# Retrieval layer of a four-stage model kernel: last product in three reduced passes, part of the vector work moved to GpSimd

## The chip, the cores and the metric

The kernel runs on one core of one Trainium2 chip. The metric is the device time of one launch in microseconds. Before the change it was 1889.96 us, the median of three runs (1884.06 to 1893.62).

## What is computed

The model has four layers over 2048 tokens of width 256, each followed by an addition and a layer normalisation. The change touches only the fourth, a retrieval layer ("product keys"). Cut to its core:

```
h   = (silu(x @ W_up.T + b_up)) @ W_down.T + b_down          # 2048 x 128
sim = q(h) against 2 x 8 sets of 45 keys                      # q(h) = h @ W_q.T
sx, ix = top 8 of the first set of each head; sy, iy = of the second
all_scores = sx[:, None] + sy[None, :]                        # 8 x 8 candidates for each head
sc, pk  = top 8 of the 64 candidates; indices = ix * 45 + iy of the chosen
z   = silu((h . down_embed[indices]) * softmax(sc))           # 64 values for each token
out = sum over the 64 of z * up_embed[indices]                # up_embed: 2048 x 256, f32
x   = layernorm(x + out)
```

## The kernel before, in words

The tokens are taken in 16 tiles of 128. Nothing is gathered by address. The 2048 experts are laid out as a grid of 16 rows by 128 columns, and an index is split into its column b and its row a. TensorE first multiplies h with the whole of down_embed (`fill_z`, `lower_z`, kept as three bf16 parts in `z`), picks the 64 columns of each token by products with one-hot matrices `is_b` (`gather`), picks the row with `of_a` on VectorE (`weigh`), and after the silu goes the way back: `spread` holds the 64 weights, each cut into three bf16 parts (`c_parts`), placed at its row by `of_a`; `scatter` multiplies them with the one-hot `of_b`; `flip` transposes; ScalarE copies the result to `W`, a 128 x 2048 f32 matrix of weights for the tile (`copy_W`); and `product` multiplies `W` with `up` (the up_embed table in SBUF), 16 products of 128 x 128 by 128 x 256 in f32, which add up in `ps_out`.

The order is written out by hand as one loop over I on each engine, with the stages of several tiles in flight. On TensorE, iteration I does: gather(I), a piece of h for a later block (`private_product`), product(I-1, part 0), select(I), the fill of z for tile I+1 with product parts 1 to 3 of tile I-1 in between, scatter(I), scores(I+3), flip(I), and, in the first iterations, another piece of h (`rise_product`). On VectorE, iteration I does:

```
marks(I)           # is_b x4 (L2147), of_a (L2138), of_b x2 (L2131)
normalize(I + 1)   # softmax sum, reciprocal, weights w (L2260 to L2264)
top_eights(I + 2)  # 16 MAX8 (L2191)
keep_h(I + 2)
weigh(I)           # masked x2 (L2160), row sum (L2163), times w (L2165)
places_of(I + 2)   # 16 FIND_INDEX8 (L2197), then cand (L2200) and the cast of the places (L2205)
cut(I)             # c_rest, c_parts (L2170 to L2174), then spread x4 (L2182)
bests(I + 2)       # 8 MAX8 (L2211), soft (L2215), 8 FIND_INDEX8 (L2219)
look_up(I + 2)     # 12 small instructions, among them hit and found (L2225 to L2256)
add_out(I - 1)
```

Engines wait for each other by counting semaphores. The instructions named above as is_b, of_a, of_b, spread, hit and found read bf16 from SBUF and write bf16 to SBUF. GpSimd has no instruction in this layer. The first token block's h comes from `private_phase`, which ends before the retrieval block begins; the tables (`down`, `up` and smaller ones) are loaded during it.

Of the kernel before, what the change touches and what calls it, by code (L numbers as in the profile page):

```python
# [1644 lines left out]
def private_phase(nc, M, D, h, wk, wu, wd, bu, bd, load_tables):  # L1645


    with scope(nc, "pv") as s:
# [9 lines left out]
        h_product, k_product = s.sem("h_product"), s.sem("k_product")  # L1658

        with nc.Block() as block:  # L1660
# [31 lines left out]
            @block.scalar  # L1692
            def _(act):
                act.wait_ge(k_product, 1)
                for n in range(2):
                    nc.scalar.activation(wk[:, n * RHEADS * KEYS:(n + 1) * RHEADS * KEYS],
                                         ps_k[n][:, 0:RHEADS * KEYS], ACT.Copy)
                act.wait_ge(up_loaded, 4 * 16)
                for m in range(UPT):
# [9 lines left out]
def retrieval_phase(nc, M, D):

    with scope(nc, "re") as s:
# [60 lines left out]
        W = s.sb("W", [P, ROWS, P])  # L1772
        masked = s.sb("masked", [P, ROWS, TWIN])
# [7 lines left out]
        lifted = s.sb("lifted", [P, QT, P])  # L1781
# [4 lines left out]
        def lane(q):  # L1786
            return wheel[:, q * BLK:(q + 1) * BLK]
# [10 lines left out]
                 "b_stored b_spread is_b_ready of_b_ready of_a_ready z_filled z_ready gathered masked_ready "  # L1798
                 "zs_ready c_ready spread_ready scattered W_ready pull selected lift flipped up_product up_ready h_used h_kept out_product added spread root normed step").split()
# [19 lines left out]

        def cut_order(j, n):  # L1820

            return (j // 2) * 2 * PARTS + n * 2 + j % 2 + 1

        with nc.Block() as block:
# [23 lines left out]
            def _(pe):  # L1848
# [268 lines left out]
            def _(dve):  # L2117
# [18 lines left out]
                def of_as(T):  # L2136
                    after(dve, "spread_ready", T * 2)
# [17 lines left out]
                def weigh(T):  # L2155
                    dve.wait_ge(S["of_a_ready"], T + 1)
                    for c in range(2):
                        after(dve, "selected", T * 2 + c + 1)
                        t = slice(c * HALF_TWIN, (c + 1) * HALF_TWIN)
                        nc.vector.tensor_tensor(masked[:, :, t], lane(c).rearrange("p (t a) -> p a t", a=ROWS),  # L2160
                                                of_a[:, :, t], ALU.mult).then_inc(S["masked_ready"], 1)
                    dve.wait_ge(S["masked_ready"], T * 2 + 2)
                    then(nc.vector.tensor_reduce(zs[:, :], masked[:, :, :].rearrange("p a t -> p t a"), AX.X, ALU.add))  # L2163
# [3 lines left out]
                def cut(T):  # L2167
# [6 lines left out]
                    then(nc.vector.tensor_tensor(c_parts[:, 2, :], c_rest[:, :], c_parts[:, 1, :], ALU.subtract))  # L2174
                    now()
                    dve.wait_ge(S["step"], 1)
                    shape = [TWIN, PARTS, ROWS, HALF_TWIN]
                    for c in range(2):
                        t = slice(c * HALF_TWIN, (c + 1) * HALF_TWIN)
                        for half in range(2):  # L2180
                            p = slice(half * TWIN, (half + 1) * TWIN)
                            last = nc.vector.tensor_tensor(  # L2182
                                spread[p, :, half * ROWS:(half + 1) * ROWS, t],
                                of_a[p, :, t].unsqueeze(1).broadcast_to(shape),
                                c_parts[p, :, t].unsqueeze(2).broadcast_to(shape), ALU.mult)
                        last.then_inc(S["spread_ready"], 1)

                def top_eights(T):
# [3 lines left out]
                    then(last)  # L2192

                def places_of(T):
                    now()
# [3 lines left out]
                    both = top[:, :, :].rearrange("p (h a) k -> p h a k", a=2)  # L2199
                    nc.vector.tensor_tensor(  # L2200
                        cand[:, :, :, :],
                        both[:, :, 0, :].unsqueeze(3).broadcast_to([P, RHEADS, K_HEAD, K_HEAD]),
                        both[:, :, 1, :].unsqueeze(2).broadcast_to([P, RHEADS, K_HEAD, K_HEAD]), ALU.add)
                    dve.wait_ge(S["sim_read"], T + 1)
                    then(nc.vector.tensor_copy(place16[:, :, :, :],  # L2205
                                               place[:, :, :].rearrange("p (h a) k -> p a k h", a=2)))
# [16 lines left out]
                def look_up(T):  # L2223
# [11 lines left out]
                    now()  # L2235
                    then(nc.vector.tensor_tensor(found[:, :, :, :].rearrange("p a i (k h) -> p (a i) k h", h=RHEADS),
# [192 lines left out]
```

## Time and profile before

| | |
|---|---|
| profiled execution, device time | 1888.3 us |
| span of the profiled execution, first to last instruction | 1886.5 us |
| median of the timed runs | 1889.96 us |
| TensorE busy over the span | 1696.0 us (90%) |
| VectorE busy over the span | 1162.3 us (62%) |
| ScalarE busy over the span | 879.1 us (47%) |
| GpSimd busy over the span | 555.1 us (29%), none of it in the retrieval layer |
| retrieval loop, first MEMSET of VectorE to the last instruction | 1321.7 to 1886.5 us |

The span is cut into engines and lines of the kernel; a row of the trace gives the start of an instruction (or of a run of like instructions), its length, its engine and line, and what it writes and reads. The shares of the whole span mix four layers with different limits, so the retrieval layer has to be read from its own stretch. The profiled execution lies 1.7 us under the median of the timed runs.

### The profile page before, as it was taken

To read this page: it belongs to the slowest core of one execution; us is meant where nothing else is said; L and a number is where in the kernel's file an instruction comes from. 1 tells how busy PE (TensorE), PEld (TensorE's weight loads), DVE (VectorE), ACT (ScalarE), POOL (GpSimd) and SP (SyncE) were. 2 spreads that over 40 slices of the span, in tenths; PEclk is the share of its full clock that TensorE was granted. 3 is DMA by queue.
4 is the path that set the end of the run, shared out by engine and by line. 5 is a ranking of instruction groups with operands and counts; after the bars stand their busy time and mean duration, and the time that the engine had idled before them with its cause. 6 is when DMAs were issued, how large, how long until landed. Compare 5 with 4: busy or idle time off the path is not lost. (4 is left out here: it accounts for less than half of the span.)

```text
span 1886.5 us, 41922 instructions
## 1 busy us (share of the span) xinstructions
PE 1696.0 (90%) x16332; PEld 1321.6 (70%) x16332; DVE 1162.3 (62%) x2902; ACT 879.1 (47%) x1576; POOL 555.1 (29%) x467
## 2 busy tenths in 40 slices
PE   7999999999999897699997987667899999899998
PEld 6888888888888686487766664224477786677777
DVE  1034434444343476223799989990898798799994
ACT  4433233333333343355776665432465555456563
POOL 2223423333342600730677878540000000000000
PEclk9999999999999899799999988897999999999999
DMA  2000000000000300622544544344212112112120
GB/s 95 19 1 26 21 4 25 25 11 14 25 22 3 114 1 3 215 89 70 169 134 145 158 127 113 105 103 127 91 47 92 47 47 86 64 47 93 59 92 24
DMA packets 74788, 129.98 MB, mean 69 GB/s; under 512 B 13520, under 2 KB 40272, under 8 KB 72408
## 3 DMA queue, kind: packets, MB, share of 16 engines
q1 hardware_dynamic: 73532, 126.09, 21.4%
q10 hardware_dynamic: 1116, 1.98, 0.3%
q8 instruction: 93, 1.52, 0.3%
q14 instruction: 47, 0.39, 0.1%
HBM read 125.28 MB, written 2.77 MB: 68 GB/s over the span
## 5 line engine op out<-in xcount | busy, mean ns | idle before, releaser
L1285 POOL TENSOR_TENSOR mo_sb_bx<-mo_sb_dtx,mo_sb_bs 128x1024 f32<-128x1024 f32 x64 | 153.3, 2396 | 87.9 <-DMA mo_sb_bs<-mo_bc 34.8
L541 POOL TENSOR_TENSOR g_sb_squares_sum<-g_sb_squares_sum,at_sb_qT 128x512 f32<-128x512 f32 x64 | 81.8, 1278 | 309.9 <-ACT at_sb_qT L472 309.9
L2045 ACT ACTIVATE re_sb_z<-re_ps_misc 128x512 bf16<-128x512 f32 x192 | 107.4, 594 | 128.9 <-PE re_ps_misc L1859 85.9
L1472 DVE TENSOR_TENSOR mo_ps_h<-mo_ps_h,mo_sb_gate 128x512 f32<-128x512 f32 x100 | 69.6, 696 | 116.1 <-ACT mo_ps_h L1321 116.0
L1480 DVE TENSOR_TENSOR_SCAN mo_ps_a<-mo_ps_a,mo_sb_bx 128x512 f32<-128x512 f32 x104 | 123.1, 1216 | 0.8 <-POOL mo_sb_bx L1285 0.5
L1946 PE MATMUL re_ps_out<-re_sb_up,re_sb_W 128*128 128x256 f32 x512 | 122.1, 383 | 0.9 <-ACT re_sb_W L2030 0.9
L503 DVE COPY at_sb_state<-at_ps_state_sum 128x128 f32<-128x128 f32 x64 | 18.6, 290 | 168.8 <-PE at_ps_state_sum L417 168.8
L1946 PEld LDWEIGHTS re_ps_out<-re_sb_up,re_sb_W 128*128 128x128 f32 x512 | 96.9, 193 | 20.1 <-issue 5.7
L512 DVE SCALAR_TENSOR_TENSOR g_sb_gated<-at_ps_out,at_sb_nw,g_sb_gated 128x512 f32 x64 | 48.1, 751 | 94.3 <-ACT at_sb_qT L472 94.3
L1334 ACT ACTIVATE mo_sb_gatedL<-mo_ps_h 128x512 fp32r<-128x512 f32 x100 | 59.9, 599 | 92.4 <-PE mo_ps_h L1151 92.0
L1142 PE MATMUL mo_ps_h<-mo_sb_xH,mo_sb_w1H 128*128 128x512 f32 x200 | 89.1, 446 | 12.6 <-DVE all_sb_x_part L1466 8.7
L472 ACT ACTIVATE at_sb_qT<-at_ps_out 128x512 f32<-128x512 f32 x64 | 38.2, 597 | 127.4 <-PE at_ps_out L433 127.4
L1402 ACT ACTIVATE mo_ps_a<-mo_sb_dt,mo_sb_decay 128x512 f32<-128x512 f32 x104 | 71.3, 693 | 48.5 <-DVE mo_sb_hc L1492 48.1
L1299 POOL TENSOR_TENSOR mo_sb_y<-mo_sb_y,mo_sb_hc 128x1024 f32<-128x1024 f32 x38 | 93.8, 2468 | 0.0
L1905 PEld LDWEIGHTS re_ps_wheel<-re_sb_is_b,re_sb_z 128*32 128x32 bf16 x3072 | 71.7, 198 | 26.6 <-issue 26.6
L1905 PE MATMUL re_ps_wheel<-re_sb_is_b,re_sb_z 128*32 128x128 bf16 x3072 | 74.8, 257 | 16.9 <-issue 16.4
L497 DVE TENSOR_TENSOR at_sb_weights<-at_ps_score,at_sb_tbl 128x512 f32<-128x512 f32 x128 | 81.9, 681 | 5.1 <-PE at_ps_score L404 5.1
L1162 PE MATMUL mo_ps_acc<-mo_sb_gatedH,mo_sb_w2H 128*128 128x512 f32 x200 | 81.1, 406 | 2.6 <-DVE all_sb_xT L1498 2.6
L1217 PE MATMUL mo_ps_acc<-mo_sb_hc,all_sb_ident 128*128 128x512 f32 x92 | 52.8, 705 | 34.0 <-DVE mo_sb_hc L1492 31.2
L458 ACT ACTIVATE at_sb_kT<-at_ps_k 128x512 f32<-128x512 f32 x64 | 38.3, 599 | 94.8 <-PE at_ps_k L378 94.8
L447 ACT ACTIVATE at_sb_v<-at_ps_v 128x256 f32<-128x256 f32 x128 | 42.2, 381 | 85.1 <-PE at_ps_v L360 85.0
L1163 PE MATMUL mo_ps_acc<-mo_sb_gatedL,mo_sb_w2H 128*128 128x512 f32 x200 | 81.2, 406 | 0.0
(275 smaller groups left out, 4771.4 us busy)
## 6 DMA issues: line engine op xcount, KB each, us to landing
re_sb_b_all<-re_b SPq DMA_DIRECT2D x16, 2048.0 KB, 8.3
mo_sb_bs<-mo_bc SPq DMA_DIRECT2D x64, 256.0 KB, 4.1
mo_sb_cs<-mo_bc SPq DMA_DIRECT2D x64, 256.0 KB, 4.2
mo_sb_gate<-mo_gates SPq DMA_DIRECT2D x36, 256.0 KB, 3.3
mo_sb_w<-in_w_dram SPq DMA_DIRECT2D x10, 640.0 KB, 9.2
at_sb_w<-in_qkv_w_dram SPq DMA_DIRECT2D x18, 256.0 KB, 3.1
mo_sb_gate<-mo_gates SPq DMA_DIRECT2D x20, 192.0 KB, 2.7
mo_sb_gate<-mo_gates SPq DMA_DIRECT2D x16, 224.0 KB, 3.1
```

The source lines that it names most:

```text
L497: nc.vector.tensor_tensor(weights[:, h, :].rearrange("p (t q) -> p t q", t=CHUNKS), ps_score[h][:, :].rearrange("p (t q) -> p t q", t=CHUNKS),
L541: nc.gpsimd.tensor_tensor(part, part, qT[n][:, :], ALU.add).then_inc(summed, 1)
L1142: nc.tensor.matmul(ps_h[n % NP][:, :], w1H[:, c, fs], xH[i % 2][:, c, :], start=(c == 0), stop=False)
L1162: nc.tensor.matmul(to, w2H[:, f, of], gatedH[n % NH][:, :], start=(f == 0), stop=False)
L1163: nc.tensor.matmul(to, w2H[:, f, of], gatedL[n % 2][:, :], start=False, stop=False)
L1285: nc.gpsimd.tensor_tensor(bx[l % 2][:, :, :], dtx[:, :, :], bs[l % NS][:, :].unsqueeze(1).broadcast_to([P, KD, BLK]), ALU.mult).then_inc(b ...
L1299: nc.gpsimd.tensor_tensor(y[i % 2][:, :, :], to, hc[l % 2][:, :, :], ALU.add).then_inc(y_added, 1)
L1402: nc.scalar.activation(bank[:, :], dt[i % 2][:, d, :], ACT.Exp, scale=decay[:, d, n:n + 1]).then_inc(a_ready, 1)
L1480: nc.vector.tensor_tensor_scan(bank[:, :], bank[:, :], bx[l % 2][:, d, :], 0.0, ALU.mult, ALU.add).then_inc(scanned, 1)
L1905: last = nc.tensor.matmul(wheel[g * 2 * ROWS:(g + 1) * 2 * ROWS, j * P:(j + 1) * P], z[:, n, :, :, token].rearrange("p a r -> p (a r)"), i ...
L1946: last = nc.tensor.matmul(ps_out[:, 0:DM], W[:, a, :], up[:, a, :], start=(a == 0), stop=(a == ROWS - 1))
L2045: nc.scalar.activation(z[:, n, :, 4 * j:4 * j + 4, :], misc[j % 2][:, :].rearrange("p (r a t) -> p a r t", r=4, a=2), ACT.Copy).then_inc(S ...
```

## The change

1. `product` now takes `W` and `up` as two parts each, a high part in the FP32R type (`WH`, `upH`) and the rest (`WL`, `upL`, which are written over `W` and `up`), and does three FP32R products for each of the 16 rows: high by high, high by rest, rest by high. 48 products of 256 columns take the place of 16 in f32.
2. GpSimd makes the parts: once, at the start of the retrieval block, `upH` and `upL` in four pieces of 128 x 1024; and for each tile `WH` and `WL` in four pieces of 128 x 512 (a cast, then a subtraction that waits for it), after the last `copy_W` of the tile.
3. GpSimd also does the sum of candidates (`cand`) and the cast of the places (`place16`), and two of the four `spread` instructions of a tile (those of the second half of the tokens' slots, `c = 1`). VectorE keeps the other two. The second half of `scatter` waits for GpSimd's.
4. `masked` is stored with the 16 rows of a slot next to each other, so that the row sum reads neighbours; the multiplication before it now reads `of_a` with a step of 64 elements.
5. Room: `found` shares the buffer of `hit`, `lifted` that of `pulled`; `k_product` shares the semaphore of `up_product`.

The core of the diff:

```diff
+        up, upL = s.sb_both("up", [P, ROWS, DM])
+        upH = s.sb("upH", [P, ROWS, DM], FP32R)
...
+        W, WL = s.sb_both("W", [P, ROWS, P])
+        WH = s.sb("WH", [P, ROWS, P], FP32R)
+        masked = s.sb("masked", [P, TWIN, ROWS])
...
+        def spread_part(engine, c, half):
+            shape = [TWIN, PARTS, ROWS, HALF_TWIN]
+            t = slice(c * HALF_TWIN, (c + 1) * HALF_TWIN)
+            p = slice(half * TWIN, (half + 1) * TWIN)
+            return engine.tensor_tensor(spread[p, :, half * ROWS:(half + 1) * ROWS, t],
+                                        of_a[p, :, t].unsqueeze(1).broadcast_to(shape),
+                                        c_parts[p, :, t].unsqueeze(2).broadcast_to(shape), ALU.mult)
...
                 def scatter(T, q):
-                    after(pe, "spread_ready", T * 2 + q // 2 + 1)
+                    if q < 2:
+                        after(pe, "spread_ready", T + 1)
+                    else:
+                        after_pool(pe, "spread", T, 1)
...
                 def product(T, part):
                     if part == 0:
-                        after(pe, "W_ready", (T + 1) * QUARTERS)
                         after(pe, "added", T)
+                    after_pool(pe, "WL", T, part)
                     for a in range(part * ROWS // 4, (part + 1) * ROWS // 4):
-                        last = nc.tensor.matmul(ps_out[:, 0:DM], W[:, a, :], up[:, a, :],
-                                                start=(a == 0), stop=(a == ROWS - 1))
+                        nc.tensor.matmul(ps_out[:, 0:DM], WH[:, a, :], upH[:, a, :], start=(a == 0), stop=False)
+                        nc.tensor.matmul(ps_out[:, 0:DM], WH[:, a, :], upL[:, a, :], start=False, stop=False)
+                        last = nc.tensor.matmul(ps_out[:, 0:DM], WL[:, a, :], upH[:, a, :], start=False,
+                                                stop=(a == ROWS - 1))
...
+            @block.gpsimd
+            def _(pool):
+                pool.wait_ge(tables_loaded, TABLES * 16)
+                for part in range(QUARTERS):
+                    r = of_part(part)
+                    nc.gpsimd.tensor_copy(upH[:, r, :], up[:, r, :]).then_inc(S["pool_step"], 1)
+                    after_pool(pool, "upH", part)
+                    nc.gpsimd.tensor_tensor(upL[:, r, :], up[:, r, :], upH[:, r, :].bitcast(FP32), ALU.subtract
+                                            ).then_inc(S["pool_step"], 1)
+                def candidates(T):
+                    pool.wait_ge(S["for_pool"], FOR_POOL["top", T])
+                    after(pool, "split_ready", T)
...
+                    nc.gpsimd.tensor_tensor(
+                        cand[:, :, :, :], ..., ALU.add).then_inc(S["pool_step"], 1)
+                    pool.wait_ge(S["sim_read"], T + 1)
+                    nc.gpsimd.tensor_copy(place16[:, :, :, :], ...).then_inc(S["pool_step"], 1)
+                def spread_late(T):
+                    pool.wait_ge(S["for_pool"], FOR_POOL["parts", T])
...
+                    for half in range(2):
+                        spread_part(nc.gpsimd, 1, half).then_inc(S["pool_step"], 1)
+                        after_pool(pool, "spread", T, half)
+                def cut_W(T):
+                    after(pool, "W_ready", (T + 1) * QUARTERS)
+                    for part in range(QUARTERS):
+                        r = of_part(part)
+                        nc.gpsimd.tensor_copy(WH[:, r, :], W[:, r, :]).then_inc(S["pool_step"], 1)
+                        after_pool(pool, "WH", T, part)
+                        nc.gpsimd.tensor_tensor(WL[:, r, :], W[:, r, :], WH[:, r, :].bitcast(FP32), ALU.subtract
+                                                ).then_inc(S["pool_step"], 1)
+                for I in range(-2, TILES + 1):
+                    if live(I + 2):
+                        candidates(I + 2)
+                    if live(I):
+                        spread_late(I)
+                        cut_W(I)
...
                 def weigh(T):
-                        nc.vector.tensor_tensor(masked[:, :, t], lane(c).rearrange("p (t a) -> p a t", a=ROWS),
-                                                of_a[:, :, t], ALU.mult).then_inc(S["masked_ready"], 1)
+                        then(nc.vector.tensor_tensor(masked[:, t, :], lane(c).rearrange("p (t a) -> p t a", a=ROWS),
+                                                     of_a[:, :, t].rearrange("p a t -> p t a"), ALU.mult))
...
                 def cut(T):
-                    for c in range(2):
-                        t = slice(c * HALF_TWIN, (c + 1) * HALF_TWIN)
-                        for half in range(2):
...
+                    spread_part(nc.vector, 0, 0)
+                    spread_part(nc.vector, 0, 1).then_inc(S["spread_ready"], 1)
...
                 def bests(T):
-                    now()
+                    after_pool(dve, "cand", T)
```

## Rows read from the trace of the kernel before

**Rows 1.** Busy time by stretch, retrieval tiles 0 to 9, then 10 to 13.
```profile
core 0: us, PE busy (x) PEld busy (x) DVE busy (x) ACT busy (x) POOL busy (x), PEclk, DMA share, GB/s
1356.00:1689.00 333.00, 311.97 (x5316) 244.42 (x5316) 285.16 (x1076) 186.82 (x345) 0.00 (x0) 0.98 0.18 67
1689.00:1823.00 134.00, 124.26 (x2436) 106.57 (x2434) 129.57 (x499) 82.85 (x156) 0.00 (x0) 1.00 0.19 70
```

**Rows 2.** Timeline of tile 11, from W of tile 10 to tile 12's is_b.
```profile
1730.13 2.06 ACT L2030 ACTIVATE re_sb_W<-re_ps_wheel 128x512 f32<-128x512 f32 x4
...
1732.71 2.73 DVE L2147 TENSOR_SCALAR re_sb_is_b<-re_sb_b_all,re_sb_own 128x2048 bf16<-128x2048 bf16 x4
...
1735.95 4.48 DVE L2131 TENSOR_TENSOR re_sb_of_b<-re_sb_rows,re_sb_splitT 128x4096 bf16<-128x4096 bf16 x2
...
1744.00 1.91 DVE L2163 TENSOR_REDUCE re_sb_zs<-re_sb_masked 128x64 f32<-128x1024 f32 x1
...
1748.89 0.68 DVE L2200 TENSOR_TENSOR re_sb_cand<-re_sb_top 128x512 f32<-128x512 f32 x1
...
1750.39 3.87 DVE L2182 TENSOR_TENSOR re_sb_spread<-re_sb_of_a,re_sb_c_parts 64x1536 bf16<-64x1536 bf16 x4
...
1755.46 0.23 DVE L2215 TENSOR_TENSOR re_sb_soft<-re_sb_best 128x64 f32<-128x64 f32 x1
...
1762.19 2.73 DVE L2147 TENSOR_SCALAR re_sb_is_b<-re_sb_b_all,re_sb_own 128x2048 bf16<-128x2048 bf16 x4
```

**Rows 3.** Timeline of DVE: is_b of tile 0 and of tile 14.
```profile
1355.80 2.75 DVE L2147 TENSOR_SCALAR re_sb_is_b<-re_sb_b_all,re_sb_own 128x2048 bf16<-128x2048 bf16 x4
...
1822.60 2.73 DVE L2147 TENSOR_SCALAR re_sb_is_b<-re_sb_b_all,re_sb_own 128x2048 bf16<-128x2048 bf16 x4
```

**Rows 4.** Timeline of PE: the last tile's product; twelve FP32R products, first and last.
```profile
1873.47 7.17 PE L1946 MATMUL re_ps_out<-re_sb_up,re_sb_W 128*128 128x256 f32 x32 [0.90 <-ACT re_sb_W L2030]
...
202.00 0.28 PE L358 MATMUL at_ps_v<-at_sb_wvH,all_sb_x_part 128*128 128x256 f32 x1
...
203.30 0.28 PE L360 MATMUL at_ps_v<-at_sb_wvH,all_sb_xT_part 128*128 128x256 f32 x1
```

**Rows 5.** Groups of POOL instructions: busy us, mean ns of one, idle before.
```profile
L271 POOL TENSOR_TENSOR at_sb_w_part<-at_sb_w,at_sb_wH 128x512 fp32r<-128x512 f32 x18 | 23.0, 1279 | 3.0 <-POOL at_sb_wH L269 2.9
...
L269 POOL CAST at_sb_wH<-at_sb_w 128x512 fp32r<-128x512 f32 x18 | 11.1, 614 | 0.0
```

**Rows 6.** Timeline of the third layer, POOL and DVE together; then L1555's ns min/median/max.
```profile
998.52 2.91 POOL L1285 TENSOR_TENSOR mo_sb_bx<-mo_sb_dtx,mo_sb_bs 128x1024 f32<-128x1024 f32 x1 [1.16 <-issue]
999.20 3.31 DVE L1555 TENSOR_TENSOR mo_sb_dt<-mo_sb_dt,mo_sb_y 128x1024 f32<-128x1024 f32 x1
...
1001.39 3.33 POOL L1299 TENSOR_TENSOR mo_sb_y<-mo_sb_y,mo_sb_hc 128x1024 f32<-128x1024 f32 x1
...
1002.62 3.19 DVE L1558 TENSOR_TENSOR mo_sb_dt<-mo_sb_log,mo_sb_dt 128x1024 f32<-128x1024 f32 x1
...
L1555 DVE TENSOR_TENSOR mo_sb_dt<-mo_sb_dt,mo_sb_y x4: 1224/2267/3312, 905.4 to 1200.0; 128x1024 f32<-128x1024 f32 x4
```

**Rows 7.** Timeline of the third layer, four DVE instructions in a run beside POOL.
```profile
1138.36 2.40 POOL L1285 TENSOR_TENSOR mo_sb_bx<-mo_sb_dtx,mo_sb_bs 128x1024 f32<-128x1024 f32 x1 [2.29 <-issue]
...
1139.00 4.92 DVE L1541 TENSOR_SCALAR all_sb_x<-all_sb_x,mo_sb_mv,mo_sb_rstd 128x256 f32<-128x256 f32 x4
1140.71 2.40 POOL L1299 TENSOR_TENSOR mo_sb_y<-mo_sb_y,mo_sb_hc 128x1024 f32<-128x1024 f32 x1
```

**Rows 8.** Timeline of the third layer, a DVE instruction with one input in PSUM (ps).
```profile
1060.00 1.22 DVE L1480 TENSOR_TENSOR_SCAN mo_ps_a<-mo_ps_a,mo_sb_bx 128x512 f32<-128x512 f32 x1
1060.07 2.40 POOL L1299 TENSOR_TENSOR mo_sb_y<-mo_sb_y,mo_sb_hc 128x1024 f32<-128x1024 f32 x1
```

**Rows 9.** Groups of DVE instructions before 1290 us: a row sum over neighbours.
```profile
L908 DVE TENSOR_REDUCE ro_sb_total<-ro_sb_kept 128x16 f32<-128x256 f32 x1 | 0.4, 420 | 0.0
```

**Rows 10.** Timeline of the start of the retrieval block on DVE: its first instruction, the first cand.
```profile
1321.73 2.62 DVE L2304 MEMSET re_sb_spread<- 128x3072 uint32 x1 [41.72 <-PEq L1660]
...
1332.48 0.67 DVE L2200 TENSOR_TENSOR re_sb_cand<-re_sb_top 128x512 f32<-128x512 f32 x1
```

More of the change, by code:

```diff
@@ L1818, in group, with count, after_pool, of_part @@
             return slice(NORM_STARTS[g], NORM_ENDS[g] + 1)
+        POOL_STEPS, FOR_POOL = {}, {}
+        def count(table, *step):
+            table[step] = len(table) + 1
+        for part in range(QUARTERS):
+            count(POOL_STEPS, "upH", part)
+            count(POOL_STEPS, "upL", part)
+        for I in range(-2, TILES + 1):
+            if live(I + 2):
+                count(FOR_POOL, "top", I + 2)
+                count(POOL_STEPS, "cand", I + 2)
+                count(POOL_STEPS, "place", I + 2)
+            if live(I):
+                count(FOR_POOL, "parts", I)
+                for half in range(2):
+                    count(POOL_STEPS, "spread", I, half)
+                for part in range(QUARTERS):
+                    count(POOL_STEPS, "WH", I, part)
+                    count(POOL_STEPS, "WL", I, part)
+        def after_pool(eng, *step):
+            if step in POOL_STEPS:
+                eng.wait_ge(S["pool_step"], POOL_STEPS[step])
+        def of_part(part):
+            return slice(part * ROWS // QUARTERS, (part + 1) * ROWS // QUARTERS)
         def cut_order(j, n):
             return (j // 2) * 2 * PARTS + n * 2 + j % 2 + 1
+        def spread_part(engine, c, half):
[5 more added lines that the diff above has]
+                                        c_parts[p, :, t].unsqueeze(2).broadcast_to(shape), ALU.mult)
         with nc.Block() as block:
@@ L2063, in silu @@
                     after(act, "zs_ready", T + 1)
-                    after(act, "spread_ready", T * 2)
+                    after(act, "spread_ready", T)
+                    after_pool(act, "spread", T - 1, 1)
                     nc.scalar.activation(c_parts[:, 0, :], zs[:, :], ACT.Silu).then_inc(S["c_ready"], 1)
@@ L2136, in of_as @@
                 def of_as(T):
-                    after(dve, "spread_ready", T * 2)
+                    after_pool(dve, "spread", T - 1, 1)
+                    after(dve, "spread_ready", T)
                     nc.vector.tensor_tensor(of_a[:, :, :], wide[:, :, :],
@@ L2159, in weigh @@
                         t = slice(c * HALF_TWIN, (c + 1) * HALF_TWIN)
[L2160 to L2163 removed]
+                        then(nc.vector.tensor_tensor(masked[:, t, :], lane(c).rearrange("p (t a) -> p t a", a=ROWS),
+                                                     of_a[:, :, t].rearrange("p a t -> p t a"), ALU.mult))
+                    now()
+                    then(nc.vector.tensor_reduce(zs[:, :], masked[:, :, :], AX.X, ALU.add))
                     now()
@@ L2173, in cut @@
                     now()
-                    then(nc.vector.tensor_tensor(c_parts[:, 2, :], c_rest[:, :], c_parts[:, 1, :], ALU.subtract))
-                    now()
+                    nc.vector.tensor_tensor(c_parts[:, 2, :], c_rest[:, :], c_parts[:, 1, :], ALU.subtract
+                                            ).then_inc(S["for_pool"], 1)
+                    dve.wait_ge(S["for_pool"], FOR_POOL["parts", T])
                     dve.wait_ge(S["step"], 1)
-                    shape = [TWIN, PARTS, ROWS, HALF_TWIN]
-                    for c in range(2):
-                        t = slice(c * HALF_TWIN, (c + 1) * HALF_TWIN)
-                        for half in range(2):
[L2181 to L2186, printed above, removed]
+                    spread_part(nc.vector, 0, 0)
+                    spread_part(nc.vector, 0, 1).then_inc(S["spread_ready"], 1)
                 def top_eights(T):
@@ L2191, in top_eights @@
                         last = nc.vector.max(top[:, q, :], sim[:, q, :])
-                    then(last)
+                    last.then_inc(S["for_pool"], 1)
                 def places_of(T):
-                    now()
+                    dve.wait_ge(S["for_pool"], FOR_POOL["top", T])
                     for q in range(2 * RHEADS):
@@ L2198, in places_of @@
                     last.then_inc(S["sim_read"], 1)
[L2199 to L2206, printed above, removed]
                 def bests(T):
-                    now()
+                    after_pool(dve, "cand", T)
                     for q in range(RHEADS):
```

30 lines of the change are left out of this document (21 added, 9 removed).

## The prediction

> **What bounds the kernel now.** I read the page first, but its shares mix four layers, so I cut the retrieval layer into stretches [rows 1]. In tiles 0 to 9 TensorE works 312 of 333 us and VectorE 285: TensorE sets the pace with VectorE close behind. In tiles 10 to 13, where no pieces of h are left to compute, VectorE works 129.6 of 134 us and is the bound. GpSimd works 0 us in both. Then I read one VectorE-bound tile in order of time [rows 2]: its period is 1762.19 - 1732.71 = 29.5 us. The whole of tiles 0 to 13 takes 1822.60 - 1355.80 = 466.8 us [rows 3], 33.3 us a tile; tiles 14, 15 and the tail take 1886.5 - 1822.6 = 63.9 us. Third, I looked in the earlier layers, where GpSimd does work, for what its work does to VectorE. That decides the forecast.
>
> **Two engines that take turns.** In [rows 6] GpSimd's first instruction runs from 998.52 to 1001.43. VectorE's sum, recorded at 999.20, takes 3.31 us where it takes 1.22 undisturbed, and ends at 1002.51, 1.08 us after GpSimd's end: it stood until GpSimd was done. GpSimd's next one takes 3.33 and ends at 1004.72; VectorE's next stood again and ends 1.09 us later, at 1005.81. So each waits for the whole instruction of the other, and they alternate. In [rows 7] this happens within a run of four VectorE instructions that need nothing from each other: GpSimd's second instruction starts at 1140.71 and takes its full 2.40 us, and VectorE's run is stretched to 4.92. VectorE gives way between two instructions. In [rows 8] the VectorE instruction has one input in PSUM, and neither it (1.22) nor GpSimd's (2.40) is stretched. So what collides with a GpSimd instruction that reads SBUF is a VectorE instruction with two SBUF inputs, or a TENSOR_SCALAR from SBUF to SBUF. In retrieval these are is_b, of_a, of_b, w, zs, cut, spread, soft and most of look_up. MAX8, FIND_INDEX8 and the row sum have one input, masked and add_out one in PSUM; I take them as free.
>
> No row shows the collision for 16-bit tiles, and is_b, of_a, of_b and spread are 16-bit. I take the f32 rows as the nearest. The Trainium skill (SBUF — State Buffer, "Who interferes with whom") says that a VectorE instruction with two SBUF inputs, or in a two-port mode, contends with a GpSimd instruction that reads SBUF, that the lock is exclusive, and makes no exception for 16 bits; the trace agrees for f32 (3.31 against 1.22). By that rule the sum is the slower one below (1986); if 16-bit tiles were free it would be the rival's 1876.
>
> **The change, part by part.**
>
> *Three passes.* The f32 product is 32 recorded passes in 7.17 us [rows 4]. FP32R products of the same 256 columns start every (203.30 - 202.00)/11 = 0.118 us, so 48 take 5.7: 1.5 us less per tile at the tail's price, and no more than that where TensorE is the bound.
>
> *Cutting W on GpSimd.* The same shape has prices: cast 0.61, subtraction 1.28, 0.16 between (2.9/18) [rows 5], so four pieces take 4 x 1.89 + 4 x 0.16 = 8.2 us. It starts when copy_W ends, at 1730.13 + 2.06 = 1732.19, half a microsecond before VectorE's is_b. So it meets is_b x4 (2.73), of_a (0.5) and of_b x2 (4.48), all colliding. In turns, from is_b's start as 0: cast to 0.1; is_b to 0.8; subtraction 2.1; is_b 2.8; cast 3.4; is_b 4.1; subtraction 5.4; is_b 6.0; cast 6.7; of_a 7.2; subtraction 8.4; of_b 10.7; cast 11.3; of_b 13.5; then the last subtraction holds w until 14.8. Before, of_b ended at 1735.95 + 4.48, or 7.7; VectorE loses 5.8 us there and about 0.8 at w (two short instructions lie between): 6.6. gather waits for is_b and moves from 2.7 to 6.0, but select still comes before VectorE asks for it at about 16.6. The pieces are ready at 2.1, 5.4, 8.4 and 14.8; TensorE asks for the first after gather (about 7) and for the others later, so the new wait in product holds nothing, select behind it included.
>
> *cand and cast on GpSimd.* From cand's start to spread's are 1.50 us [rows 2], half of them cut's three small instructions; VectorE saves about 0.76. GpSimd's cand takes 1.28 and lies beside masked, the row sum and FIND_INDEX8. The cast of places stands before c_rest: at most 0.6, I take 0.3.
>
> *Row sum.* 1.91 us for 1024 elements in steps [rows 2]; 256 neighbours took 0.42 [rows 9], four times that is 1.68: at least 0.2 gained. But masked now reads of_a in steps, two of 512, which could lose 0.7 if a step costs there what it cost the row sum. Net between -0.7 and +0.7; I take -0.3.
>
> *Half of spread on GpSimd.* VectorE has four in 3.87, 0.97 each. On GpSimd there is no bf16 row; by f32, 512 elements 1.28 and 1024 2.40, 2.19 ns an element, so 1536 take 3.5 (an estimate). Lower bound: the cast's price, 3 x 0.61 = 1.8; upper: 3 x 1.28 = 3.8. I take 3.5, since it too has two inputs. Both engines wait for the same c_parts and then alternate: VectorE 0.97, GpSimd 3.5, VectorE 0.97: 5.4 instead of 3.9 (+1.5). GpSimd's second starts there and runs 3.5; soft, wanted 1.2 after spread (1755.46 against 1754.26), stands until its end: +2.3. scatter's second half waits too: the fourth spread ends at 8.9 instead of 3.9 after c_parts. Queued behind it on TensorE are scores, flip and rise_product, and behind these copy_W; W comes again about when VectorE ends its tile, so the next cut of W meets is_b once more.
>
> Sum for a VectorE-bound tile: +6.6 - 0.8 + 0.3 - 0.3 + 1.5 + 2.3 = +9.6, a period of 39.1 us. TensorE's tile (33.3 less 1.5) is then below VectorE's, so the product's gain hides and tiles 0 to 9 take 39.1 as well: 14 x 39.1 = 547, against 466.8: **+81**.
>
> *Tiles 14, 15 and the tail.* No top-8 work is left; the path runs through spread, scatter and W: +5.0 for each of two tiles; the last product waits for all of cut W, 8.2, plus a last quarter 1.4, against 7.17: +2.4. **+12**.
>
> *The start.* GpSimd cuts `up` first, from 1321.7 [rows 10]: four casts of 1024 (at most 1.2) and subtractions (2.40), with gaps 15.0, to 1336.7; cand(0) then to 1338.0, where before it was done at 1333.2. The start is a chain with nothing beside it: **+4** net of the cand time saved in the next tile.
>
> *At nothing:* shared buffers and the shared semaphore; each writer already came after the last reader on the same path.
>
> 1888.3 + 81 + 12 + 4 = 1985.3, **1986 us**. The profiled execution is 1.7 below the median, which I leave.
>
> **The rivals.**
> *A, faster: 16-bit tiles don't collide.* For it: no row shows that they do. Against: the rule of two SBUF inputs held for every f32 form found. VectorE then saves 0.8 + 1.9 + 0.3 = 3.0 in tiles 10 to 13 (-12); tiles 0 to 9 gain 1.2 to 1.5 on TensorE (-13); start +4; end +3 for each tile's late spread, +2.4. Sum -10: 1876. It decides if of_b keeps its 2.24 us.
> *B, no change: VectorE doesn't give way inside a run.* Then cut W waits until after of_b, and costs 1 us under w; spread's two run together (-1.9), soft and look_up wait 3.8. VectorE's tile is about 31.6, below TensorE's 32 to 33: tiles 0 to 9 -12, 10 to 13 +8, start and end +12: 1896. Against it: [rows 7].
> *C, slower by less: GpSimd's bf16 spread is cheap.* At 1.8, a tile loses 3.4 less: 16 x 3.4 = 54, so 1932.
> *D, slower by more.* keep_h (ten of the tiles) and the normalisation (two), left out of the 39.1, may add some 10 (an estimate: one wide instruction each time, or four); short rows of 32 elements may cost GpSimd more; and TensorE, now waiting in each tile, may be granted 1.2 GHz in stretches. 2030 to 2050.
>
> **How the numbers follow.** My forecast (1960 to 2020) 0.54, C 0.19, D 0.07, A 0.14, B 0.06. A measurement of this kernel can tell about 0.5%, 9 us. Faster is A: 0.14. B is half within it: same 0.05. Slower 0.81. The likeliest one's own range is 1960 to 2020; to hold 8 in 10, the range takes in C and part of D, and reaches down to B: 1895 to 2030.
>
> **What would show it.** In the profile after: of_b and is_b with means well over 2.24 and 0.7 us; GpSimd busy some 16 us a tile; the is_b of two tiles 37 to 41 us apart; VectorE's spread near 0.95 once and near 4.4 once; soft near 2.5 instead of 0.23; TensorE idle before scatter's second half; cand(0) late by 4 to 5 us. Wrong if of_b stays at 2.24 beside a busy GpSimd, if GpSimd's spread takes far from 3.5, or if W comes so late that cut W falls on MAX8 and FIND_INDEX8, where it is free.

## The result, and the profile after

The changed kernel takes 1947.04 us, the median, against 1889.28 for the kernel before on the same chip: ratio 1.0299, interval 1.0274 to 1.0324. It is slower. (One run of 3901.57 us, at a clock of 0.42, is left out.) The forecast was 1986 in a range of 1895 to 2030: the sign was right, and the loss of 58 us was 0.6 of the 97 forecast. 1947 lies in that range, but below the 1960 to 2020 that the prediction gave as its own forecast's.

The profiled run took 1943.97 us, with a span of 1942.2. Its row that answers to [rows 10], and its rows that answer to [rows 3], from VectorE's timeline (start, length, engine, line, output <- input, count):

```profile
1322.71 2.62 DVE L2382 MEMSET re_sb_spread<- 128x3072 uint32 x1 [41.66 <-PEq L1660]
...
1356.50 2.74 DVE L2239 TENSOR_SCALAR re_sb_is_b<-re_sb_b_all,re_sb_own 128x2048 bf16<-128x2048 bf16 x4
...
1720.32 4.21 DVE L2239 TENSOR_SCALAR re_sb_is_b<-re_sb_b_all,re_sb_own 128x2048 bf16<-128x2048 bf16 x4
...
1868.53 4.92 DVE L2239 TENSOR_SCALAR re_sb_is_b<-re_sb_b_all,re_sb_own 128x2048 bf16<-128x2048 bf16 x4
```

Starts such as these cut every kernel below into the same four stretches, counted from the block's first MEMSET, so that the layers ahead, whose length differs by some us from run to run, fall out (us; each a difference of two starts in that kernel's profile, the last one the span's end less a start):

| | MEMSET to tile 0 | tiles 0 to 9 | tiles 10 to 13 | 14 to the end | sum |
|---|---|---|---|---|---|
| before | 34.1 | 345.9 | 120.9 | 63.9 | 564.8 |
| after | 33.8 | 363.8 | 148.2 | 73.7 | 619.5 |
| e1 spread back on VectorE | 33.8 | 340.2 | 133.5 | 69.5 | 577.0 |
| e2 f32 product, nothing cut | 33.1 | 340.4 | 129.7 | 67.0 | 570.3 |
| e3 zero fills for the cutting | 33.8 | 338.2 | 136.9 | 68.2 | 577.0 |
| e4 cut late | 33.8 | 340.3 | 132.4 | 69.9 | 576.4 |
| e5 cut late, spread back | 33.8 | 335.9 | 120.9 | 64.2 | 554.8 |
| e6 f32 product, spread back | 30.5 | 349.1 | 119.5 | 63.1 | 562.2 |
| e7 as e5, old masked | 33.8 | 335.3 | 121.0 | 65.1 | 555.1 |
| e8 spread one after the other | 33.8 | 385.5 | 152.1 | 77.8 | 649.1 |

The windows of the kernel after, which answer to [rows 1] (busy us and number of instructions by engine):

```profile
core 0: us, PE busy (x) PEld busy (x) DVE busy (x) ACT busy (x) POOL busy (x), PEclk, DMA share, GB/s
1356.00:1683.00 327.00, 293.88 (x5136) 239.23 (x5135) 320.56 (x977) 177.21 (x327) 186.94 (x101) 0.96 0.16 62
1683.00:1868.50 185.50, 149.62 (x2826) 130.76 (x2824) 181.70 (x545) 94.18 (x174) 111.65 (x62) 0.90 0.17 62
```

VectorE is now recorded as busy for 98% of both windows (tiles 0 to 8, and 9 to 13), and TensorE has time left. VectorE's busy time has grown although work was taken from it, so its instructions must have become longer. The granted clock of TensorE is lower than before (0.90 in the second window, where tiles 10 to 13 had 1.00 [rows 1]), but with VectorE recorded as busy for 98% TensorE doesn't set the pace there. Of all its waits in tiles 0 to 13, this is the only line that names a result of GpSimd (us in total, times, longest):

```profile
PE re_ps_wheel L1970 <- POOL re_sb_spread L1859: 2.0, 4, 0.6
```

The groups of VectorE's instructions in the retrieval block (busy us, mean ns of one) show which:

```profile
L2222 DVE TENSOR_TENSOR re_sb_of_b<-re_sb_rows,re_sb_splitT 128x4096 bf16<-128x4096 bf16 x32 | 93.1, 2947 | 0.0
L1859 DVE TENSOR_TENSOR re_sb_spread<-re_sb_of_a,re_sb_c_parts 64x1536 bf16<-64x1536 bf16 x32 | 78.5, 2453 | 0.9 <-DVE re_sb_c_parts L2266 0.2
L2239 DVE TENSOR_SCALAR re_sb_is_b<-re_sb_b_all,re_sb_own 128x2048 bf16<-128x2048 bf16 x64 | 71.2, 1173 | 0.0
L2252 DVE TENSOR_TENSOR re_sb_masked<-re_ps_wheel,re_sb_of_a 128x512 f32<-128x512 f32 x32 | 32.0, 1041 | 4.9 <-PE re_ps_wheel L1957 4.9
L2292 DVE TENSOR_TENSOR re_sb_soft<-re_sb_best 128x64 f32<-128x64 f32 x16 | 25.5, 1594 | 0.6
L2230 DVE TENSOR_TENSOR re_sb_of_a<-re_sb_wide,re_sb_splitT 128x1024 bf16<-128x1024 bf16 x16 | 21.3, 1330 | 0.0
L2255 DVE TENSOR_REDUCE re_sb_zs<-re_sb_masked 128x64 f32<-128x1024 f32 x16 | 19.5, 1220 | 0.5
```

The same groups before: of_b 2286, spread 953, is_b 747, masked 687, soft 226, of_a 685, row sum 1910 ns. (masked and the row sum were edited themselves.) Now one tile in order of time, the one that starts at 1758.54; GpSimd's rows first, then VectorE's:

```profile
1758.41 0.62 POOL L2091 CAST re_sb_WH<-re_sb_W 128x512 fp32r<-128x512 f32 x1 [10.09 <-ACT re_sb_W L2120]
1759.11 1.62 POOL L2093 TENSOR_TENSOR re_sb_W_part<-re_sb_W,re_sb_WH 128x512 fp32r<-128x512 f32 x1
...
1766.19 2.67 POOL L2091 CAST re_sb_WH<-re_sb_W 128x512 fp32r<-128x512 f32 x1
1768.94 3.19 POOL L2093 TENSOR_TENSOR re_sb_W_part<-re_sb_W,re_sb_WH 128x512 fp32r<-128x512 f32 x1
...
1780.94 7.68 POOL L1859 TENSOR_TENSOR re_sb_spread<-re_sb_of_a,re_sb_c_parts 64x1536 bf16<-64x1536 bf16 x2 [0.39 <-DVE re_sb_c_parts L2266]
```

```profile
1758.54 5.52 DVE L2239 TENSOR_SCALAR re_sb_is_b<-re_sb_b_all,re_sb_own 128x2048 bf16<-128x2048 bf16 x4
1763.98 1.11 DVE L2230 TENSOR_TENSOR re_sb_of_a<-re_sb_wide,re_sb_splitT 128x1024 bf16<-128x1024 bf16 x1
1765.02 5.99 DVE L2222 TENSOR_TENSOR re_sb_of_b<-re_sb_rows,re_sb_splitT 128x4096 bf16<-128x4096 bf16 x2
...
1771.41 0.80 DVE L2342 TENSOR_TENSOR re_sb_w<-re_sb_soft,re_sb_total 128x64 f32<-128x64 f32 x1
1772.14 1.80 DVE L2276 MAX8 re_sb_top<-re_sb_sim 128x8 f32<-128x45 f32 x16
...
1780.89 4.74 DVE L1859 TENSOR_TENSOR re_sb_spread<-re_sb_of_a,re_sb_c_parts 64x1536 bf16<-64x1536 bf16 x2
1785.66 1.11 DVE L2288 MAX8 re_sb_best<-re_sb_cand 128x8 f32<-128x64 f32 x8
1786.81 1.89 DVE L2292 TENSOR_TENSOR re_sb_soft<-re_sb_best 128x64 f32<-128x64 f32 x1
```

GpSimd's casts and subtractions, 0.61 and 1.28 us in [rows 5], are 2.67 and 3.19 beside of_b, and of_b is 5.99 for two instead of 4.48 [rows 2]. The last subtraction ends at 1772.13, and w, a 0.23 us instruction, ends at 1772.21: it stood until then. GpSimd's spread ends at 1788.62, and soft at 1788.70. The eight MAX8 of 1785.66, beside GpSimd's spread, keep the 1.11 us that they took before.

### The profile page after: what moved, and what is told of

It reads as the page before. It is cut to its first block and busy times, and to the rows that moved or that the text cites. A ratio compares the mean times of both kernels' runs of the same rounds, so it can differ in the third digit from the quotient of the medians.

```text
span 1942.2 us, 42633 instructions
## 1 busy us (share of the span) xinstructions
PE 1701.4 (88%) x16588; PEld 1340.3 (69%) x16588; DVE 1258.1 (65%) x2838; ACT 879.1 (45%) x1576; POOL 912.5 (47%) x667
## 5 line engine op out<-in xcount | busy, mean ns | idle before, releaser
L2091 POOL CAST re_sb_WH<-re_sb_W 128x512 fp32r<-128x512 f32 x64 | 81.0, 1266 | 113.4 <-ACT re_sb_W L2120 113.4
L1859 POOL TENSOR_TENSOR re_sb_spread<-re_sb_of_a,re_sb_c_parts 64x1536 bf16<-64x1536 bf16 x32 | 121.2, 3787 | 16.4 <-DVE re_sb_c_parts L2266 15.1
L2093 POOL TENSOR_TENSOR re_sb_W_part<-re_sb_W,re_sb_WH 128x512 fp32r<-128x512 f32 x64 | 120.7, 1887 | 5.1
L1905 PE MATMUL re_ps_misc<-re_sb_z,re_sb_minus 128*128 128x512 bf16 x128 | 47.4, 412 | 56.3 <-ACT re_sb_z L2135 55.2
L472 ACT ACTIVATE at_sb_qT<-at_ps_out 128x512 f32<-128x512 f32 x64 | 38.2, 598 | 127.4 <-PE at_ps_out L433 127.4
L2222 DVE TENSOR_TENSOR re_sb_of_b<-re_sb_rows,re_sb_splitT 128x4096 bf16<-128x4096 bf16 x32 | 93.1, 2947 | 0.0
L1988 PE MATMUL re_ps_out<-re_sb_upH,re_sb_WH 128*128 128x256 f32 x256 | 84.4, 330 | 4.0 <-POOL re_sb_W_part L2093 3.8
L1970 PEld LDWEIGHTS re_ps_wheel<-re_sb_of_b,re_sb_spread 128*32 128x32 bf16 x3072 | 73.5, 196 | 17.5 <-DVE re_sb_spread L1859 10.2
L1970 PE MATMUL re_ps_wheel<-re_sb_of_b,re_sb_spread 128*32 128x128 bf16 x3072 | 76.6, 261 | 10.0 <-DVE re_sb_spread L1859 7.8
```

The lines of the kernel that those rows point to most:

```text
L1859: return engine.tensor_tensor(spread[p, :, half * ROWS:(half + 1) * ROWS, t], of_a[p, :, t].unsqueeze(1).broadcast_to(shape), c_parts[p, : ...
L1970: last = nc.tensor.matmul(wheel[g * 2 * ROWS:(g + 1) * 2 * ROWS, j * P:(j + 1) * P], spread[:, n, :, token], of_b[token // HALF_TWIN][:, t ...
L1988: nc.tensor.matmul(ps_out[:, 0:DM], WH[:, a, :], upH[:, a, :], start=(a == 0), stop=False)
L2093: nc.gpsimd.tensor_tensor(WL[:, r, :], W[:, r, :], WH[:, r, :].bitcast(FP32), ALU.subtract).then_inc(S["pool_step"], 1)
L2222: nc.vector.tensor_tensor(of_b[c][:, :, :, :], rows[:, :, :].unsqueeze(1).broadcast_to(shape), splitT[T % 2][:, 0, t].rearrange("p (t k) - ...
```

## The experiments

Two theories stood against each other after the result. *Turns*, the prediction's: what VectorE loses is standing (waiting until the other engine's instruction has ended, which the profile records as a longer instruction), in the two places where it and GpSimd want the same instructions' time (cut W beside is_b, of_a, of_b and w; spread beside spread and soft). *Late results*: W's parts and the fourth spread come later from the slower engine, and TensorE and what follows wait for them.

**e1, all four spread on VectorE again.**

```diff
-                    for half in range(2):
-                        spread_part(nc.gpsimd, 1, half).then_inc(S["pool_step"], 1)
...
+                    spread_part(nc.vector, 1, 0)
+                    spread_part(nc.vector, 1, 1).then_inc(S["spread_ready"], 1)
```

> The changed kernel with all four spread instructions on VectorE again; GpSimd keeps cand, the cast of places and the cutting of up and W. Theory 'turns' (what costs is that VectorE's instructions with two SBUF inputs and GpSimd's stand for each other): per tile the four spreads take 3.9 us in place of 4.7, and soft falls from 1.59 to 0.23, so a tile is 2.2 us shorter, 36.9 to 34.7; with the two late tiles, about 1907 us. Rival 'late results' (what costs is that scatter's second half and product wait for GpSimd, and VectorE's stretched instructions are cover): scatter's second half comes 3.8 us earlier after c_parts, so a tile loses up to 3.8, 1944 - 16 x 3.8 = 1883 us.

Measured 1902.29 us, ratio to before 1.0062 (1.0043 to 1.0082). Spread is back at 953 ns and soft at 227; of_b stays at 2812, is_b at 966. Giving GpSimd half of spread cost 45 us in the changed kernel.

**e2, the f32 product of before, nothing cut; spread still shared.**

```diff
-                        nc.tensor.matmul(ps_out[:, 0:DM], WH[:, a, :], upH[:, a, :], start=(a == 0), stop=False)
-                        nc.tensor.matmul(ps_out[:, 0:DM], WH[:, a, :], upL[:, a, :], start=False, stop=False)
...
+                        last = nc.tensor.matmul(ps_out[:, 0:DM], W[:, a, :], up[:, a, :],
+                                                start=(a == 0), stop=(a == ROWS - 1))
...
-                        cut_W(I)
```

> The changed kernel with the f32 product of before, so that GpSimd cuts neither up nor W; cand, the cast of places and half of spread stay on GpSimd. 'Turns': is_b, of_a, of_b and w return to 2.7, 0.69, 2 x 2.24 and 0.23 us; a tile loses 4.0 to 5.3 us of VectorE's time, down to 32 to 33, where TensorE's f32 tile (33.3 before) sets the pace in tiles 0 to 9: 1944 - 10 x 3.3 - 4 x 4.5 - 3 = about 1890 us. 'Late results': TensorE stood only 4 us in all for the parts of W, and pays 1.2 us more per tile for the f32 product: 1944 - 4 + 16 x 1.2, about 1955 us.

Measured 1899.55, ratio 1.0053 (1.0036 to 1.0070). of_b 2286, is_b 747, of_a 687 are back at their times of before, and spread (2447) and soft (1594) still stand. The three passes with their cutting cost 47 us in the changed kernel. e1 and e2 came 5 and 10 us from what turns gave, and 19 and 55 from late results.

**e3, GpSimd fills in place of the cutting.**

```diff
-                        nc.gpsimd.tensor_copy(WH[:, r, :], W[:, r, :]).then_inc(S["pool_step"], 1)
+                        nc.gpsimd.memset(WH[:, r, :].bitcast(FP32), 0.0).then_inc(S["pool_step"], 1)
...
-                        nc.gpsimd.tensor_tensor(WL[:, r, :], W[:, r, :], WH[:, r, :].bitcast(FP32), ALU.subtract
-                                                ).then_inc(S["pool_step"], 1)
+                        nc.gpsimd.memset(WL[:, r, :].bitcast(FP32), 0.0).then_inc(S["pool_step"], 1)
+                        after_pool(pool, "WX", T, part)
+                        nc.gpsimd.memset(WL[:, r, :].bitcast(FP32), 0.0).then_inc(S["pool_step"], 1)
```

> The changed kernel, in which the cutting of W is left out: in place of cast and subtraction GpSimd fills each piece of WH and WL with zeros (three fills of 128 x 512 a piece, about 0.5 us each with 0.1 to 0.2 between, all waits kept), so the retrieval layer adds nothing to the output. It reads nothing from SBUF for that. If the collision is about reading SBUF: of_b and of_a keep 2.24 and 0.69 us beside the fills, a tile is 2 to 2.6 us shorter, about 1910 us; is_b may still be stretched. If any GpSimd instruction on SBUF collides: of_b stays near 2.7 to 2.9 us and the time stays within 10 us of 1944, less the shorter fills.

One run: 1899.3 us, where cutting takes 1947 (about 1910 expected). The kernel leaves out the retrieval layer's sum, since WH and WL are zero. GpSimd works in the same place, but it only writes. Three of its rows in one tile, then VectorE's beside them:

```profile
1762.02 0.52 POOL L2092 MEMSET re_sb_WH<- 128x512 f32 x1 [6.63 <-ACT re_sb_W L2122]
1762.60 0.97 POOL L2094 MEMSET re_sb_W_part<- 128x512 f32 x1
...
1767.71 0.55 POOL L2094 MEMSET re_sb_W_part<- 128x512 f32 x1
```

```profile
1761.97 4.70 DVE L2241 TENSOR_SCALAR re_sb_is_b<-re_sb_b_all,re_sb_own 128x2048 bf16<-128x2048 bf16 x4
1766.59 0.67 DVE L2232 TENSOR_TENSOR re_sb_of_a<-re_sb_wide,re_sb_splitT 128x1024 bf16<-128x1024 bf16 x1
1767.18 4.48 DVE L2224 TENSOR_TENSOR re_sb_of_b<-re_sb_rows,re_sb_splitT 128x4096 bf16<-128x4096 bf16 x2
```

A fill beside of_b takes 0.55 us, and of_b keeps 4.48. Beside is_b fills take up to 0.99, and is_b 4.70 instead of 2.73. So here VectorE's instructions with two SBUF inputs stand only for a GpSimd instruction that reads, and is_b, a TENSOR_SCALAR, for one that only writes as well. The Trainium skill (SBUF — State Buffer, "Who interferes with whom") says that two SBUF inputs contend with GpSimd's reads and not with its writes, and an instruction in a two-port mode with GpSimd altogether. The trace agrees with the first half by of_b's 4.48; by is_b's 4.70 it agrees with the second if is_b runs in such a mode, which no row names.

**e4, the cutting at another time.** GpSimd begins when VectorE has made w of the next tile, so that it runs beside MAX8, masked, the row sum and FIND_INDEX8; TensorE takes each quarter of the product one place later, and the cast of the places comes after the cutting. Spread is still shared.

```diff
-                def cut_W(T):
+                def cut_W(T, parts):
                     after(pool, "W_ready", (T + 1) * QUARTERS)
+                    if live(T + 2):
+                        after(pool, "w_ready", T + 3)
...
+                    if live(I - 1):
+                        cut_W(I - 1, range(1))
                     if live(I + 2):
                         candidates(I + 2)
+                    if live(I - 1):
+                        cut_W(I - 1, range(1, QUARTERS))
```

> The changed kernel with the cutting of W moved: GpSimd starts it after VectorE's w of the next tile (first piece, then cand, then the other three), where VectorE has MAX8, masked, the row sum and FIND_INDEX8; TensorE's four quarters of product come one place later each. GpSimd's work and half of spread stay. 'Turns': is_b, of_a, of_b, w fall back to 2.7, 0.69, 2 x 2.24, 0.5; a tile loses about 4.5 us, 36.9 to 32.4; 1944 - 13 x 4.5, about 1886 us. 'Late results': parts of W come 8 us later, TensorE waits for them more: no faster, 1944 to 1975 us.

Measured 1895.17, ratio 1.0023 (1.0009 to 1.0038). That is 9 us above what turns gave. Every part of W is made later in its tile than in the changed kernel, and the time falls by 52 us; that refutes late results for W. For spread they are refuted by e1's time, 5 us from one theory and 19 from the other, and by the 2.0 us that TensorE waited for it. of_b (2288), is_b (747) and GpSimd's cast (613) and subtraction (1277) are all undisturbed. Some of the 9 us is standing that has moved: c_rest takes 476 ns instead of 218, and the product with w before it 446 instead of 225.

**e5, both: the late cutting, and spread on VectorE.**

> W is cut beside MAX8, masked, the row sum and FIND_INDEX8, as in the late cut, and VectorE makes all four spread again. GpSimd keeps only the cutting, cand and the cast of the places. Theory of turns: the two places at which the engines meet are both gone, so tiles 0 to 9 are left with TensorE as the bound, 1.2 to 1.5 us shorter than before, and tiles 10 to 13 with VectorE at 28.9 to 30 us; the tail pays some 2 us for the last cut. Some 1872 us (1868 to 1880), faster than before. Rival, that the remaining GpSimd work (cand, place cast, cuts) or the three passes themselves cost the path something even where no such meeting shows: 1886 to 1893, no faster than before.

Measured 1873.36, ratio 0.9931 (0.9912 to 0.9950): 0.7% faster than before, and at what turns gave. Of the 14.3 us, the stretches above show 10.0 in the retrieval block, all of it in tiles 0 to 9; the rest of the profiled run's lead lies in the layers ahead, which the edit doesn't touch. In tiles 10 to 13 nothing is won (120.9), though VectorE no longer makes cand (0.67 us). One such tile, GpSimd and then VectorE:

```profile
1755.97 0.61 POOL L2090 CAST re_sb_WH<-re_sb_W 128x512 fp32r<-128x512 f32 x1 [20.65 <-DVE re_sb_w L2344]
...
1763.46 1.27 POOL L2092 TENSOR_TENSOR re_sb_W_part<-re_sb_W,re_sb_WH 128x512 fp32r<-128x512 f32 x1
```

```profile
1759.51 1.22 DVE L2255 TENSOR_REDUCE re_sb_zs<-re_sb_masked 128x64 f32<-128x1024 f32 x1
...
1763.72 1.10 DVE L2262 TENSOR_TENSOR re_sb_c_rest<-re_sb_c_whole,re_sb_c_parts 128x64 f32<-128x64 f32 x1
```

The last subtraction ends at 1764.73, and c_rest, 0.21 us where it is free, stands for it and ends at 1764.82: 0.9 us back. The free window, MAX8 to FIND_INDEX8, is just too short for the four pairs and cand.

**e6, spread on VectorE and the f32 product:** of the change only cand and the cast of the places on GpSimd are left, and the new masked.

> Nothing is cut: the last product is the f32 one of before, and VectorE makes all four spread. Of the change only the offload of cand and of the cast of the places, and the layout of masked, are left. Theory of turns: cand and the cast lie beside FIND_INDEX8, which has one input, so VectorE gains 0.8 us a tile; it counts only where VectorE is the bound (tiles 10 to 13, 3 us) and at most in part of the others: 1882 to 1887 us. If this offload itself costs (the first MAX8 of bests waits for GpSimd's cand): 1890 to 1895. If it comes as low as the late cut with spread on VectorE, the three passes bring nothing.

Measured 1881.56, ratio 0.9958 (0.9944 to 0.9973). In the retrieval block it is 2.6 us ahead of before; to tile 10 it needs 379.6 us after the MEMSET, before 380.0, and e5 369.7. e5 has the product one place later as well; e1, which has the three passes in the old place, needs 374.0, so with VectorE still standing it is 5.6 ahead of e6. So the gain of e5 is that of the three passes, about 1.0 us a tile where TensorE sets the pace, and the offload of cand by itself is worth little. e6 is 65 us faster than the changed kernel, not the 92 of e1 and e2 added up: with both gone TensorE, busy for 309 of 330 us where VectorE is for 273, sets the pace again in tiles 0 to 9.

**e7, e5 with masked stored as before**, of_a read in order and the row sum in steps.

```diff
-        masked = s.sb("masked", [P, TWIN, ROWS])
+        masked = s.sb("masked", [P, ROWS, TWIN])
```

> The late cut with spread on VectorE, and masked stored as before the change, so that of_a is read in order and the row sum in steps. From the rows of after the two masked lose 0.7 us by the new layout and the row sum gains 0.7: within 2 us of the same kernel with the new layout. If the layout did pay as the prediction had it (0.3 a tile), this one is some 4 us slower; if the row sum collides with GpSimd when it reads in steps, more.

Measured 1877.26, ratio 0.9943 (0.9923 to 0.9963); its median is 3.9 us above that of e5, as it would be if the layout paid, but the intervals overlap, and the profiled runs, 3.8 us apart, differ by only 0.3 in the retrieval block (555.1 and 554.8): the rest lies ahead of the MEMSET. The new layout is worth nothing that shows: what the row sum gains the multiplication pays (in e7 1948 and 686 ns, in e5 1220 and 1051).

**e8, GpSimd's spread alone.** VectorE begins its two when GpSimd has ended its two.

```diff
+                    after_pool(dve, "spread", T, 1)
                     spread_part(nc.vector, 0, 0)
```

> The changed kernel with one edit: VectorE starts its two spread only when GpSimd's two are done, so that the two engines never run spread together; GpSimd's two are then measured alone. Theory of turns: a recorded 3.79 us holds about 0.9 us of standing, so GpSimd's spread falls to 2.85 to 3.0 us, VectorE's to 0.95 and soft to 0.23; the stretch from c_parts to the end of soft grows from some 7.8 to some 9.1 us, 16 times: 1960 to 1972 us. Rival, that 3.79 us is what GpSimd needs by itself and VectorE alone stands: 3.79 stays, and the time is 1980 to 1995. The prediction's estimate of 3.5 would lie between.

Measured 1970.81, ratio 1.0416 (1.0390 to 1.0442), as turns gave it. The groups of GpSimd's and VectorE's spread:

```profile
L1859 POOL TENSOR_TENSOR re_sb_spread<-re_sb_of_a,re_sb_c_parts 64x1536 bf16<-64x1536 bf16 x32 | 99.3, 3105 | 12.4 <-DVE re_sb_c_parts L2266 11.1
...
L1859 DVE TENSOR_TENSOR re_sb_spread<-re_sb_of_a,re_sb_c_parts 64x1536 bf16<-64x1536 bf16 x32 | 30.5, 953 | 104.6 <-POOL re_sb_spread L1859 104.4
```

Alone it takes 3.1 us, a little more than expected (2.85 to 3.0) and less than the 3.79 recorded in the changed kernel: there some 0.7 us were standing. It is 3.3 times VectorE's 0.95. soft, which now begins after GpSimd's end, is back at 225 ns.

## Why the prediction was right, and by how much it was off

- **Two engines that take turns.** Right, and for 16-bit tiles too: of_b, of_a and spread stand as the f32 rows do. e2 gives of_b back its 2286 ns by taking GpSimd's readers away, e4 by moving them. Rival A (16-bit tiles don't collide) fell with of_b at 2947 ns, rival B (VectorE keeps its turn inside a run) with is_b at 5.52 us for four that need nothing from each other.
- **Cutting W, forecast +6.6 a tile.** From is_b's start to w's end it took 12.4 us in the tile of 1720.32 and 13.67 in that of 1758.54, against 8.4 before: +4.0 and +5.3. Mis-sized. The ends of w, before and after, and the first tile's last pair:

```profile
1740.84 0.23 DVE L2264 TENSOR_TENSOR re_sb_w<-re_sb_soft,re_sb_total 128x64 f32<-128x64 f32 x1
...
1731.90 0.81 DVE L2342 TENSOR_TENSOR re_sb_w<-re_sb_soft,re_sb_total 128x64 f32<-128x64 f32 x1
1732.63 1.80 DVE L2276 MAX8 re_sb_top<-re_sb_sim 128x8 f32<-128x45 f32 x16
...
1732.57 0.61 POOL L2091 CAST re_sb_WH<-re_sb_W 128x512 fp32r<-128x512 f32 x1
1733.26 1.28 POOL L2093 TENSOR_TENSOR re_sb_W_part<-re_sb_W,re_sb_WH 128x512 fp32r<-128x512 f32 x1
```

  The forecast had the cutting begin half a microsecond ahead of is_b; in the first of the two W came 0.9 after it, and the last pair fell on MAX8, where it is free. The prediction had named that as a way to be wrong. In the second the order was nearly the forecast's, with the first cast beginning 0.1 us ahead of is_b, and the last piece still came at 13.6 us instead of 14.8.
- **Half of spread, forecast +1.5, and soft, +2.3.** Mis-sized by the estimate of 3.5 us for GpSimd's spread; e8 has 3.1, and in the tile of 1758.54 VectorE stood 4.74 - 2 x 0.95 = 2.8 for it. VectorE's pair took 4.74 instead of four in 3.87, +0.9, and soft 1594 instead of 226 ns, +1.4. Rival C's 1932 lies nearer to the result (15 us) than my 1986 (39), but not by its working: its price of 1.8 was further from 3.1 than mine, and it kept the full price for cutting W.
- **cand, places, row sum: forecast -0.8, +0.3 and -0.3.** GpSimd's cand took 1.07 (forecast 1.28). The cast of the places makes c_parts' cast longer by 0.14 (333 ns instead of 195). Row sum and masked together gave 0.0: -0.69, where 1.22 us came for the 1.68 reckoned, and two times +0.35. A step costs the multiplication as much as it had cost the sum. e6, which keeps only these terms, gains (120.9 - 119.5)/4 = 0.35 us a tile, where -0.8 was forecast for them together.
- **The tile's sum, forecast +9.6.** Tiles 10 to 13 lost (148.2 - 120.9)/4 = 6.8 us each. The parts, 4.0 to 5.3, -0.35 (e6), 0.9 and 1.4, give 6.0 to 7.3.
- **Tiles 0 to 9.** The prediction took 1689 for the start of tile 10, which begins at 1701.73; the stretch of 333 us held 9.6 tiles, and a tile took 34.6 there and 30.2 afterwards. The sum over 14 isn't touched by that. VectorE had 333 - 285 = 48 us of slack in the 9.6 tiles [rows 1], 5.0 each. If all of it could be used, 1.8 of the 6.8 would show, and (363.8 - 345.9)/10 = 1.8 did; the exact match is partly luck, since VectorE still has 6.4 us of the first window idle. That the product's gain would hide was right; e5 and e6 show it as 1.0 us a tile once VectorE is out of the way (forecast 1.2 to 1.5).
- **The start, forecast +4.** Missed. VectorE's rows there, after:

```profile
1336.77 1.11 DVE L2288 MAX8 re_sb_best<-re_sb_cand 128x8 f32<-128x64 f32 x8 [3.22 <-POOL re_sb_cand L2071]
...
1343.78 0.21 DVE L2338 TENSOR_REDUCE re_sb_total<-re_sb_soft 128x8 f32<-128x64 f32 x1
```

  bests of the first tile waited 3.22 us for cand, where the forecast had cand 4 to 5 us late, and began at 1336.77 instead of 1333.37. But tile 0 came 33.8 us after the MEMSET instead of 34.1. The softmax sum, which before waited 1.71 us for ScalarE, now waits for nothing, and cand and its cast are gone from the next tile on VectorE: most of the delay ran into a wait that was there already, and the MEMSET itself came 1.0 later. I had called the start a chain with nothing beside it.
- **The tail, forecast +12.** 73.7 - 63.9 = 9.8. The last cutting took 7.7 us (1926.90 to 1934.62), forecast 8.2.
- **Rivals A and D in the working.** A's terms come to -12.6 with two late tiles, and 1876 follows from that, not from the -10 written beside it. Of D, the lower clock came, in tiles 10 to 13 without a price that shows; no run tells what it cost in the tail.
- **The signs named.** The is_b of tiles 10 to 14 lie 36.4 to 38.2 us apart (37 to 41 named). GpSimd's records hold 111.65 us in the five tiles of the second window, 22 a tile where 16 were named, since they hold its standing too. That TensorE would be idle before scatter's second half hardly showed (2.0 us in all).

So the step that was mis-sized is the price of the standing: a tile lost 6.8 us for 9.6, which over 14 tiles is 39 of the 42 us between the forecast loss of 97 and the 55 of the retrieval block. The one term that was wrong in kind is the start.

## What to carry to other kernels

Before work is moved from VectorE to GpSimd, look at what VectorE does at that moment: if it has two SBUF inputs, or is a TENSOR_SCALAR from SBUF to SBUF, the two take turns when GpSimd's reads SBUF, and work that takes GpSimd three times as long stands in VectorE's way for that long. Such work cost next to nothing here beside MAX8, FIND_INDEX8, the row sum or masked, which has an input in PSUM (in e5 190, 196, 1220 and 1051 ns; in e6, where nothing is cut, 190, 198, 1220 and 1041). Moving the same cutting there turned +58 us into +6, and giving spread back as well into -14. Read a longer mean of an untouched instruction as standing, and find for whose end it stood.

## What the runs showed of the hardware

- GpSimd's two-input bf16 instruction of 64 x 1536 takes 3.1 us alone, 2.0 ns an element, close to the 2.3 of f32 (2.40 us for 1024, [rows 7]): 16 bits didn't make GpSimd much faster here, where VectorE needs 0.95.
- Zero fills by GpSimd leave of_b alone (2282 ns) and hold is_b (1081 instead of 747).
- A step of 64 elements in one bf16 SBUF input took VectorE's multiplication of 128 x 512 from 687 to 1041 ns, though its other input, in PSUM, is then read in neighbours and no longer in steps of 16.
- A 0.2 us VectorE instruction can cost 0.6 to 1.7 us more when it asks while GpSimd is at work: c_rest in e5, w and soft in the changed kernel.
